# Expert tables made in seven pieces between the shared items, the first expert's weight split shared by three engines, a block transpose that writes a matrix (PSUM) bank

## The reference

```python
x = x + attention(bi_wkv(x, f, f, w1, u1, cond))        # 16 heads of 128, causal
x2 = bi_wkv(x, f, f, w2, u2, cond)                      # two scans over time, sigmoid gate
scores = sigmoid(x2 @ gate_w)                           # 2048 tokens, 32 experts
# 2 of 4 groups of experts by their best score, then 6 experts among these
g = ragged_dot(xs, w_gate); u = ragged_dot(xs, w_up)    # xs: the tokens sorted by expert
d = ragged_dot(silu(g) * u, w_down)                     # 512 -> 352 -> 512
expert_out = sum over the 6 of d * weight
shared = (silu(x2 @ sw_gate) * (x2 @ sw_up)) @ sw_down  # 512 -> 704 -> 512
out = x + expert_out + shared
```

## Time and profile before

| | |
|---|---|
| median of three runs | 2350.36 us (2345.12 to 2357.11) |
| the profiled execution's own time | 2350.14 us |
| its span, first to last instruction | 2348.4 us |
| busy share of the span | PE 91%, DVE 61%, ACT 50%, POOL 62% |
| mean granted TensorE clock | 0.961 of full speed |

### The profile page before, as it was taken

How to read it: one execution, slowest core, us unless ns; L and a number is a source line. 1 busy time by engine, 2 the same in 40 slices (tenths; PEclk the granted TensorE clock), 3 DMA queues, 4 the chain that set the end, 5 groups by cost and what they waited for, 6 DMA issues and landing times. The chain is left out here.

```text
span 2348.4 us, 39884 instructions
## 1 busy us (share of the span) xinstructions
PE 2147.8 (91%) x11247; PEld 1865.5 (79%) x11247; DVE 1437.7 (61%) x2499; ACT 1162.6 (50%) x2490; POOL 1466.3 (62%) x963
## 2 busy tenths in 40 slices
PE   2889999999999989898788788999999999999996
PEld 1678888888878878777677677988899999998974
DVE  7868878778856676767755334434445454544386
ACT  4467777777767767667552113333333333333310
POOL 7877787787755656567561304556778787753355
PEclk6989999999999999999897899999999999999998
DMA  5434444533365545665335624555666676654666
GB/s 126 142 107 126 135 133 159 163 118 101 123 221 162 157 150 182 207 193 187 100 123 211 213 76 142 156 155 168 185 189 208 185 207 190 197 184 141 179 203 196
DMA packets 368184, 381.33 MB, mean 162 GB/s; under 512 B 51572, under 2 KB 283576, under 8 KB 363256
## 3 DMA queue, kind: packets, MB, share of 16 engines
q1 hardware_dynamic: 256136, 253.25, 35.1%
q10 hardware_dynamic: 96496, 75.28, 10.4%
q0 software_dynamic: 15360, 50.34, 6.5%
HBM read 265.26 MB, written 121.63 MB: 165 GB/s over the span
## 5 line engine op out<-in xcount | busy, mean ns | idle before, releaser
L2023 POOL TENSOR_SCALAR we_high<-we_raw 128x1408 fp32r<-128x1408 f32 (+1 forms) x95 | 153.1, 1612 | 305.0 <-PE up_e L670 208.6
L2025 POOL TENSOR_TENSOR we_low<-we_raw,we_high 128x1408 fp32r<-128x1408 f32 (+1 forms) x95 | 321.4, 3383 | 7.9
L2214 DVE TENSOR_TENSOR hT_low<-hT_ps,hT_high 128x256 fp32r<-128x256 f32 x127 | 53.9, 424 | 247.9 <-ACT hT_high L2159 243.5
L2171 ACT ACTIVATE silu_e<-gate_e 128x352 f32<-128x352 f32 x127 | 59.0, 465 | 285.9 <-PE up_e L670 274.1
L670 PE MATMUL gate_e<-we_high,xT_high 128*128 x508 | 176.1, 347 | 16.7 <-DVE xT_low L2221 9.9
L2227 DVE TENSOR_TENSOR hidden_e<-silu_e,up_e 128x352 f32<-128x352 f32 x127 | 66.0, 520 | 194.9 <-ACT silu_e L2171 194.8
L2176 ACT ACTIVATE rows_out<-down_e 128x512 f32<-128x512 f32 x127 | 75.9, 598 | 195.8 <-PE down_e L670 192.4
L670 PE MATMUL gate_e<-we_high,xT_low 128*128 x508 | 164.4, 324 | 0.0
L670 PE MATMUL gate_e<-we_low,xT_high 128*128 x508 | 163.9, 323 | 0.0
L670 PE MATMUL up_e<-we_high,xT_high 128*128 x508 | 163.9, 323 | 0.0
L670 PE MATMUL up_e<-we_high,xT_low 128*128 x508 | 163.7, 322 | 0.0
(11 more groups left out here) (388 smaller groups left out, 7207.7 us busy)
## 6 DMA issues: line engine op xcount, KB each, us to landing
slots_out<-rows_out ACTq DMA_DIRECT2D x127, 256.0 KB
rows_early<-slots_in ACTq DMA_DIRECT2D x500, 64.0 KB
we_raw<-L_ffn_w_gate SPq DMA_DIRECT2D x32, 704.0 KB, 4.7
we_raw<-L_ffn_w_up SPq DMA_DIRECT2D x32, 704.0 KB, 5.2
w_ring<-L_attn_Wq SPq DMA_DIRECT2D x64, 256.0 KB
q_T<-q_out SPq DMA_DIRECT2D x64, 256.0 KB, 2.4
w_ring<-L_attn_Wk SPq DMA_DIRECT2D x64, 256.0 KB
w_ring<-L_attn_Wv SPq DMA_DIRECT2D x64, 256.0 KB
```

Of the source, the lines that this page charges most:

```text
L2023: nc.gpsimd.tensor_scalar(wh[:, p, at:to], raw[:, at:to], 1.0, 1.0, ALU.mult, ALU.mult).then_inc(w_hi, 1)
L2025: nc.gpsimd.tensor_tensor(wl[:, p, at:to], raw[:, at:to], wh[:, p, at:to].bitcast(F32), ALU.subtract).then_inc(w_split, 1)
```

## The change

1. The expert tables are cut into pieces: `sizes`, `places`, `experts_in_order`, `blocks_in_order`, `rows_of_blocks`, `slot_shifts` and `block_table`. The region ends are still copied at once; the pieces then stand ahead of DVE's products of items 4, 5, 6, 7, 8, 9 and 11. The instructions are the same, but for a fill of the row table that goes. The six `final_slots` stand ahead of items 10, 13, 14, 15, 17 and 18. SP's wait before the row loads asks for item 11's product in place of item 12's.
2. ACT splits the first shared weights between its copies of the last x2 chunk, not after the scores.
3. The first expert: ACT and DVE make the gate part, POOL the up part, at the stage's start, and then POOL the down part. PE's first gate products wait for the former, its first up products for the latter. Two of the signals that let SP load the next expert's gate and up parts come together after both.
4. The block transpose writes a PSUM bank (`psx`, which only the sums used) in place of SBUF; ACT's high half and DVE's low half read it there. One bank serves all blocks; a transpose waits for the low half of the block before, which is earlier in DVE's own stream.
5. `high(0)` and `low(0)` move from the start of the stage behind step 3.

```diff
+SLOTS_AT = (10, 13, 14, 15, 17, 18)
-            sp.wait_ge(h_dve, B * (3 - POOL_ITEMS) + 1)
+            sp.wait_ge(h_dve, 11 - B * POOL_ITEMS + 1)
...
                 nc.scalar.activation(x2h[:, B - 1, c, :], x2[:, c, :], ACT.Copy).then_inc(x2_hi, 1)
+                if c == KC - 1:
+                    split_high(0)
...
-            split_high(0)
...
-            nc.vector.memset(xrow[:], ZERO_ROW)
...
             for i in range(B * POOL_ITEMS, len(items)):
                 m, b = items[i]
                 if b == 0 and 1 < m + 1 < len(SCH):
                     split_low(m + 1)
+                if i == 4:
+                    sizes()
+                elif i == 5:
+                    places()
+                elif i == 6:
+                    experts_in_order()
+                elif i == 7:
+                    blocks_in_order()
+                elif i == 8:
+                    rows_of_blocks()
+                elif i == 9:
+                    slot_shifts()
+                elif i == 11:
+                    block_table()
+                elif i in SLOTS_AT:
+                    final_slots(SLOTS_AT.index(i))
+                gated(i)
...
-                        if i == 1:
-                            pool.sem_inc(w_hi, 1)
-                            pool.wait_ge(part_lo, CHUNKS + KC + 1)
-                            pool.wait_ge(w_split, len(W_PARTS) + 2)
-                            pool.sem_inc(w_split, 1)
-                            pool.wait_ge(w_split, len(W_PARTS) + 3)
+                        if i < 2:
                             continue
-                        pool.wait_ge(we_in, 64)
...
+            pool.wait_ge(we_in, 64)
+            pool.sem_inc(pool_steps, 1)
+            nc.gpsimd.tensor_scalar(wh[:, 0, W_UP:W_DOWN], raw[:, W_UP:W_DOWN], 1.0, 1.0, ALU.mult, ALU.mult).then_inc(w_hi, 1)
+            pool.wait_ge(w_hi, 1)
+            nc.gpsimd.tensor_tensor(wl[:, 0, W_UP:W_DOWN], raw[:, W_UP:W_DOWN], wh[:, 0, W_UP:W_DOWN].bitcast(F32),
+                                    ALU.subtract).then_inc(first_up, 1)
+            pool.wait_ge(part_lo, CHUNKS + KC + 1)
+            pool.wait_ge(first_up, 1)
+            pool.sem_inc(w_hi, 1)
+            pool.sem_inc(w_split, 2)
             split(0, 0, None)
...
-                        pe.wait_ge(w_split, len(W_PARTS) + 2)
+                        pe.wait_ge(part_lo, CHUNKS + KC + 1)
...
-                            pe.wait_ge(w_split, 2 * len(W_PARTS))
+                            pe.wait_ge(first_up, 1)
...
-            high(0)
             act.wait_ge(we_in, 64)
-            nc.scalar.activation(wh[:, 0, W_UP:W_DOWN], raw[:, W_UP:W_DOWN], ACT.Copy).then_inc(part_hi, 1)
+            nc.scalar.activation(wh[:, 0, 0:W_UP], raw[:, 0:W_UP], ACT.Copy).then_inc(part_hi, 1)
...
-                    nc.scalar.activation(xth[:, p, :, :], xt[:, p, :].rearrange("p (k t) -> p k t", k=KC), ACT.Copy).then_inc(x_hi, 1)
+                    nc.scalar.activation(xth[:, p, :, :], psx[:].rearrange("p (k t) -> p k t", k=KC), ACT.Copy).then_inc(x_hi, 1)
...
+                if n == 3:
+                    high(0)
...
-            low(0)
-
             def transpose_rows(n):
                 p = n % 2
                 dve.wait_ge(xg_in[p], 16 * NQD * (n // 2 + 1))
-                nc.vector.transpose(xt[:, p, :].rearrange("p (k i b) -> p k i b", k=KC, b=QD),
+                dve.wait_ge(x_lo, done(n - 1))
+                nc.vector.transpose(psx[:].rearrange("p (k i b) -> p k i b", k=KC, b=QD),
                                     xg[:, p, :].rearrange("p (i k a) -> p k i a", k=KC, a=QD)).then_inc(x_T, 1)
...
-                    nc.vector.tensor_tensor(xtl[:, p, :, :], xt[:, p, :].rearrange("p (k t) -> p k t", k=KC),
+                    nc.vector.tensor_tensor(xtl[:, p, :, :], psx[:].rearrange("p (k t) -> p k t", k=KC),
...
             transpose_rows(0)
-            step(written_out(0, NBLK))
             dve.wait_ge(part_hi, CHUNKS + KC + 1)
-            nc.vector.tensor_tensor(wl[:, 0, W_UP:W_DOWN], raw[:, W_UP:W_DOWN], wh[:, 0, W_UP:W_DOWN].bitcast(F32),
+            nc.vector.tensor_tensor(wl[:, 0, 0:W_UP], raw[:, 0:W_UP], wh[:, 0, 0:W_UP].bitcast(F32),
                                     ALU.subtract).then_inc(part_lo, 1)
-            for n in range(1, NBLK + 2):
+            for n in range(NBLK + 2):
                 step(written_out(n, NBLK))
+                if n == 3:
+                    low(0)
             low(1)
```

More of the change, by code:

```diff
@@ L1829, in _ @@
             cnt, iota_e = rt["cnt"], rt["iota_e"]
[L1830 to L1836, removed]
             stt = nc.vector.scalar_tensor_tensor
@@ L1848, in _ @@
[L1848 to L1862, removed]
@@ L1871, in _, with sizes @@
[L1871 to L1874, removed]
+            def sizes():
+                then(stt(out=count[:], in0=iota_e[:], scalar=-float(CAP), in1=cnt[:], op0=ALU.mult, op1=ALU.add))
+                then(tt(more, count[:].unsqueeze(2).broadcast_to([P, E, NT]), iota_q[:].unsqueeze(1).broadcast_to([P, E, NT]), ALU.is_gt))
+                then(red(nb[:], more, AX.X, ALU.add))
+                nc.vector.memset(ones_e[:], 1.0)
+                then(ts(nb[:], nb[:], 1.0, None, ALU.max))
@@ new lines, in places, with experts_in_order @@
+            def places():
+                then(stt(out=key, in0=nb[:], scalar=float(E), in1=iota_e[:], op0=ALU.mult, op1=ALU.add))
+                then(tt(pairs, across(key), down(key), ALU.is_gt))
+                then(red(pos, pairs, AX.X, ALU.add))
+                then(ts(key, pos, -2.0, float(2 * E - 1), ALU.mult, ALU.add))
+                then(stt(out=pos, in0=pos, scalar=2.0, in1=key, op0=ALU.mult, op1=ALU.min))
+            def experts_in_order():
+                then(tt(at_place, across(pos), down(iota_e[:]), ALU.is_equal))
+                then(tt(pairs, at_place, across(iota_e[:]), ALU.mult))
+                then(red(id_at, pairs, AX.X, ALU.add))
+                then(nc.vector.tensor_copy(order[:], id_at[0:1, :]))
+                dve.sem_inc(order_done, 1)
@@ new lines, in slot_shifts, with block_table @@
+            def slot_shifts():
+                then(tt(n_at, incl[:], n_at, ALU.subtract))
+                then(tt(pairs, at_place, down(n_at), ALU.mult))
+                then(red(shift[:], pairs.rearrange("p q e -> p e q"), AX.X, ALU.add))
+                then(nc.vector.tensor_scalar(shift[:], shift[:], float(P), None, ALU.mult))
+                then(stt(out=shift[:], in0=iota_e[:], scalar=-float(CAP), in1=shift[:], op0=ALU.mult, op1=ALU.add))
+            def block_table():
+                dve.wait_ge(row_mm, 1)
+                then(nc.vector.tensor_copy(ebi[:, 0, :], pst[0][0:1, 0:P]))
+                then(ts(ebi[:, 1, :], ebi[:, 0, :], 1, None, ALU.bitwise_and))
+                tab2 = tab[:].rearrange("o (b c) -> o b c", c=2)
+                ts(tab2[:, :, 0], pst[0][0:1, 0:P], 2.0, None, ALU.add)
+                nc.vector.tensor_copy(tab2[:, :, 1], ebi[:, 1, :])
+                nc.vector.tensor_copy(xrow[:, 0:P], pst[0][0:1, P:2 * P])
@@ L1894, in _ @@
                 tt(hsh[0:n, m, b * S:(b + 1) * S], sg[0:n, i % 2, :], up, ALU.mult).then_inc(h_dve, 1)
+            dve.wait_ge(consts, 2)
+            nc.vector.tensor_copy(ends[:], cnt[0:1, :]).then_inc(ends_done, 1)
+            for i in range(B * POOL_ITEMS, len(items)):
+                m, b = items[i]
+                if b == 0 and 1 < m + 1 < len(SCH):
+                    split_low(m + 1)
+                if i == 4:
[15 more added lines that the diff above has]
+                gated(i)
 W_PARTS = ((0, W_UP, 1), (W_UP, W_DOWN, 1), (W_DOWN, W_N, 2))
```

51 lines of the change are left out of this document (21 added, 30 removed).

## The result

| | before | after |
|---|---|---|
| median of 8 runs each | 2351.16 us | 2335.95 us |
| lowest to highest | 2345.12 to 2357.11 | 2332.95 to 2339.41 |
| profiled execution | 2350.14 (span 2348.4) | 2339.41 (span 2337.7) |

The ratio is 0.9939, 95% interval 0.9925 to 0.9954: 11 to 18 us faster; forecast were 2334.4 us. The profiled execution of after is the longest of its eight, so its trace shows 10.7 us of the 15. All of it stands ahead of the first expert matmul (1416.80 to 1406.02, 10.8); from there to the end of the span the two traces are equal (931.6 and 931.7 us).

The account below looks back on a forecast made before the run. TensorE, busy 91%, bounds the kernel, but SP's chain of fills would end the shared stage. 10.2 + 1.9 + 2.3 + 2.3 - 1.0 = 15.7 us off 2350.14 gives 2334.4, own range 2328 to 2342, overall 2320 to 2347.

Parts of the forecast that it names:

- (3): Shared stage's end: SP's chain of zero fills and row loads sets it, about 1398.7; 10.2 us gained, bounds 4 to 19.
- A: Rival: the fills run freely, the shared stage ends at 1390.1, time 2325.8 us; chance 0.13 together with D.
- C: Rival: later weights make more fills long, 8.3 us each; four give 2367.6 us; chance 0.06.
- D: Rival: fills don't hold the shared stage's end; gain 27.8 + 5.5 us, time 2316.8; chance 0.13 together with A.
- B: Rival: chain of fills 6 us late, POOL first at the seam, half of (5) missing; 2344.5 us; chance 0.21.
- (5): Experts' blocks, transpose into PSUM: steady xT_low saves 2.3 us of hidden_e waits and 2.3 at changes of expert.
- (2): Shared stage, tables in pieces: DVE's stalls go; a late SiLU costs 0 to 12 us, PE ends 1379 to 1391.
- undisturbed time: Shared stage: PE's end without any stall, put at 1379.1, 27.8 us earlier than before.
- (1): Shared stage's start: early split of first weights removes the 2.64 us before the first shared matmul; routing moves equally.
- (4): Seam to the first expert matmul: gain 3.7 us if DVE is first, 0.1 if POOL is; 1.9 taken.
- (6): Shared split of tile 0, moved into the fourth step, delays hT_high and hT_low: costs 0 to 3.2 us, 1.0 taken.

Follow-up runs that it names:

- scatters_one: The changed kernel, with GpSimd starting each of the last batch's 24 scatters only when the one before has landed; ratio to before 0.9942.
- psum_only: The kernel before, with the block transpose into the PSUM matrix bank alone; ratio to before 0.9987.
- fills_quick: The changed kernel, with SP reading a fill's address before it waits for the fill ahead, not after; ratio to before 0.9926.

## Why the prediction was right, point by point

**(3), the chain of fills, was right and bounds the stage.** SP's end was forecast at 1398.7 and came at 1398.49; DVE's waits at the exit (2.85, 4.88 and 16.48 us against 0.76 where SP was early) show that it holds all engines. So rivals A, C and D fell: fills neither ran freely nor got much longer (two under the scatters took 8.42 us), and they do hold the stage. Of B the seam came true, and in after's trace the missing half of (5). The order of the experts came at 1298.1 instead of 1297.1, the weights 2 us later than forecast, without effect on the chain's end. The agreement to 0.2 us is in part luck: counted from the copy, the unchanged fills ended after 112.8 to 115.1 us in the four kernels with tables in one go and after 115.2 to 117.5 in the four with pieces.

**(2), the size of the late signals, was wrong, and the time hid it.** The step put PE's end at 1379 to 1391. It came at 1394.58, 15.5 over 1379.1 and 3.6 outside the bounds. The undisturbed time was right: in `scatters_one` PE ended at 1395.44 - 25.07 = 1370.37, 97.65 us after the copy, and 1379.1 lies 97.6 behind the forecast's copy (1284.07 - 2.6). The last product follows PE's end by 1.9 us, so PE's end must stay under 1396.8, not 1398, to be hidden under the chain. The other 111.94 - 97.65 = 14.3 us are the scatters' doing: PE stood for 11.64 and restarted slowly for some 2.6.

The step that failed is the run-ahead. It had PE lose 9 us and a restart, because it let three items (6 to 8) run ahead of the late SiLU until 1308. But PE may begin item 8 only when the product of item 6 is made, so it could do two, and it stood from 1315.53 - 11.64 = 1303.89. With two, the step's own numbers give a stand from 1256.8 + 2.6 + 8 x 5.44 = 1302.9 to 1317.8, 17.5 us lost with the restart and PE's end at 1396.6, beside the chain of fills; the SiLU came 3.7 us earlier than assumed (1314.07), which took a part of that back.

In before PE stood for the tables until 1304.86, so most of the lateness fell into a stall that was there already; with the tables cut it became PE's own. The granted clock is a part of it, in the restart: 0.50, the lower of the two levels (1.2 GHz), behind PE's stall, and 0.97 again ten us later (PE first, clock third from the end):

```profile
1310.00:1320.00 10.00, 4.47 (x11) 3.53 (x12) 3.94 (x8) 1.40 (x3) 4.16 (x5) 0.50 0.91 332
1320.00:1330.00 10.00, 10.00 (x45) 8.19 (x44) 7.96 (x19) 1.93 (x3) 0.00 (x0) 0.97 0.28 107
```

So the fills set the 10.2 us, but without them the gain would have been nearly the same: the items would have ended the stage at 1396.5 and not, as rival D says, at 1379.

**(1), the early split,** took the wait of 2.64 us away; the region ends came 1.4 us earlier in this execution.

**(4), the seam, took the middle, where there is none.** GpSimd was ahead by 0.02 us and the seam fell from 7.93 to 7.53: 0.4 for 1.9. The Trainium skill, SBUF — State Buffer, section Who interferes with whom, says that issue order decides who blocks; 4.62 and 1.63 us for the same subtraction with the order turned agree.

**(5), the transpose,** was right in kind, and one of its two terms isn't shown. xT_low no longer varies, and the transpose itself costs the same (0.72 us, 0.70 before). PE's waits for GpSimd fell by 2.1 us (2.5 in `psum_only`); 2.3 were forecast. Those named for hidden_e fell by 1.7, but two waits ahead of the same PE transposes, 2.4 us, now stand as "issue". Together they are 5.2 us in after and 4.4 in `psum_only` for 4.5 in before, where 2.3 less were forecast. The tile, then the waits from 1405 us on:

```profile
L2255 DVE TENSOR_TENSOR xT_low<-xT_ps,xT_high x127: 673/677/691, 1405.1 to 2208.4; 128x512 fp32r<-128x512 f32 x127
```

```profile
PE gate_e L670 <- POOL we_low L2049: 4.7, 5, 1.0
...
PE hT_ps L2116 <- DVE hidden_e L2261: 2.8, 2, 1.7
...
PE hT_ps L2116 <- issue: 2.4, 2, 1.4
```

**(6), the moved split,** was forecast at 1.0 and cost 1.1. The block with it took 1437.67 - 1430.29 = 7.4 us where its neighbours take 6.3:

```profile
1430.29 0.52 DVE L2261 TENSOR_TENSOR hidden_e<-silu_e,up_e 128x352 f32<-128x352 f32 x1 [0.55 <-ACT silu_e L2204]
...
1437.67 0.52 DVE L2261 TENSOR_TENSOR hidden_e<-silu_e,up_e 128x352 f32<-128x352 f32 x1 [2.62 <-ACT silu_e L2204]
1443.97 0.52 DVE L2261 TENSOR_TENSOR hidden_e<-silu_e,up_e 128x352 f32<-128x352 f32 x1 [1.75 <-ACT silu_e L2204]
```

**The sum.** Of the forecast 15.7 us the two traces show 10.4 at the stage's end (for 10.2), 0.4 at the seam (for 1.9) and 1.9 in the blocks (for 3.6); behind the blocks after's execution took 2.0 longer than before's (129.3 and 127.3 us from the last xT_low to the end; 124.4 to 129.9 in all these traces). That leaves 10.7 us, where the medians show 15. The chain of fills carries the forecast. That the total came within 2 us is in part luck, since the runs don't settle what (4) to (6) are worth together.

## What to carry to other kernels

Before a stall is taken away, look at who else would end the stage: here removing one of two bounds shortened the stage by 1.7 us (`fills_quick`) or 0.7 (`scatters_one`), and both together by 16. A wait whose releaser the profile can't name deserves an experiment of its own before it gets a size, the more so where it overlaps the stall that is to go. An engine that pours out transfers long before anybody needs them should be paced, since its own time is free (GpSimd stood idle for 83.7 us behind its scatters) and that of the others isn't.

## What the runs showed of the hardware

- With 24 indirect scatters of 128 rows let go at one each 1.26 us, a SiLU whose products were made came 7 to 20 us late and PE stood behind it for 3.1 to 13.65 us; with six at a time nothing was late, at a DMA share of 0.84 in 1300 to 1320 us. In five of the six kernels PE also stood up to 2.41 us between matmuls that wait for nothing (`fills_quick`, at 1312.69), so its own instructions came late. Whether the SiLU waited for its signal or for its instruction is open.
- Reading a fill's address before the wait for the fill ahead made 16 fills take 34.06 us in place of 41.99, 0.5 us each, of SP's own time.
